# Storing a gathered row whole, in one run per partition, between two edge stages

## The reference

```
m1  = segment_sum(relu(x[src] + edge_attr), dst);             x = ln(x + (1 + eps) * x + m1)
l2  = 10 times f <- 0.9 * segment_sum(f[src] * ew, dst) + 0.1 * x;        x = ln(x + f)
h   = relu(x @ w1[r] + b1[r]) @ w2[r]
m3  = segment_sum(h[src, type] * norm, dst);                  x = ln(x + relu(m3 + b2))
e   = (x[dst] - x[src]) @ theta.T + tb + (x @ phi.T + pb)[src]
out = ln(x + segment_max(e, dst)), with 0 where a node has no edge
```

## Time and profile before

| what | value |
|---|---|
| device time, median of three runs | 4377.33 us (4374.49 to 4379.94) |
| span of the profiled execution | 4361.2 us |
| device time of that execution | not listed apart; the median is 16.1 us above the span |
| PE, DVE, ACT, POOL busy, share of the span | 56%, 66%, 31%, 60% |
| mean DMA rate | 128 GB/s |

### The profile page before, as it was taken

How to read it: one execution, slowest core, us unless ns; L and a number is a source line. 1 busy time by engine, 2 the same in 40 slices (tenths; PEclk the granted TensorE clock), 3 DMA queues, 4 the chain that set the end, 5 groups by cost and what they waited for, 6 DMA issues and landing times. The chain is left out here.

```text
span 4361.2 us, 60883 instructions
## 1 busy us (share of the span) xinstructions
PE 2429.7 (56%) x9482; PEld 1156.1 (27%) x9482; DVE 2868.7 (66%) x7411; ACT 1336.2 (31%) x4693; POOL 2603.5 (60%) x2544
## 2 busy tenths in 40 slices
PE   4720000677774888888886675642222106986564
PEld 2510000333331443344443221111111102333332
DVE  7989998788894888788887675323323144663333
ACT  0023333455552554455544221111000013431111
POOL 4747772666663777744444664756556604646776
PEclk9965555799997999899998897775555558995555
DMA  6647776899997866855553785224434242332111
GB/s 225 238 112 215 218 216 193 161 174 180 179 184 111 203 162 161 174 143 145 142 145 93 185 208 122 67 49 64 46 45 49 28 122 73 74 63 42 37 38 25
DMA packets 628412, 557.12 MB, mean 128 GB/s; under 512 B 379089, under 2 KB 548122, under 8 KB 623330
## 3 DMA queue, kind: packets, MB, share of 16 engines
q1 hardware_dynamic: 477606, 418.72, 35.7%
q0 software_dynamic: 90112, 95.44, 15.7%
q10 hardware_dynamic: 60612, 42.15, 4.6%
HBM read 291.63 MB, written 290.82 MB: 134 GB/s over the span
## 5 line engine op out<-in xcount | busy, mean ns | idle before, releaser
L1303 POOL DMA_INDIRECT out<-xob,ob x400 | 414.7, 1037 | 354.8 <-DVE xob L1415 246.8
L487 POOL DMA_INDIRECT xdst<-in_x,dstc x400 | 455.3, 1138 | 224.9 <-issue 135.0
L273 POOL DMA_INDIRECT gb<-nodes,ib x400 | 386.3, 966 | 258.0 <-ACT ib L851 141.6
L257 PE MATMUL bank<-ident,act 128*99 128x128 f32 x400 | 70.2, 302 | 657.9 <-ACT act L888 655.5
L273 POOL DMA_INDIRECT cgb<-layer,ib x160 | 175.4, 1096 | 232.4 <-ACT ib L2194 185.9
L293 PE MATMUL bank<-chosen,rec 128*6 128x512 bf16 x1200 | 309.2, 413 | 0.6 <-ACT packed L879 0.6
L1342 PE MATMUL bank<-hm,w 128*48 128x512 f32 x600 | 294.1, 629 | 0.0
L1359 PE MATMUL bank<-bxT,w 105*128 105x512 f32 x600 | 282.7, 607 | 8.5 <-ACT bxT L1246 8.5
L267 PE MATMUL bank<-ident,scan 99*128 99x99 f32 (+2 forms) x1120 | 200.2, 309 | 136.2 <-DVE scan L2013 101.5
L286 PE MATMUL bank<-l_chosen,l_rec 128*3 128x512 f32 x480 | 254.0, 679 | 0.5 <-DVE l_chosen L280 0.3
L273 POOL DMA_INDIRECT parent<-upper_rows,ib x176 | 175.3, 996 | 121.6 <-ACT ib L1271 57.1
(11 more groups left out here) (293 smaller groups left out, 6920.3 us busy)
## 6 DMA issues: line engine op xcount, KB each, us to landing
nodes<-wt SPq DMA_DIRECT2D x40, 1286.2 KB
edges<-gb ACTq DMA_DIRECT2D x100, 194.0 KB
upper_rows<-tb SPq DMA_DIRECT2D x100, 194.0 KB
xa<-upper_rows SPq DMA_DIRECT2D x100, 194.0 KB
lsb<-edges SPq DMA_DIRECT2D x100, 194.0 KB
run_rows<-upper_rows SPq DMA_DIRECT2D x100, 194.0 KB
deep_sum<-zeros SPq DMA_DIRECT2D x20, 960.0 KB
layer<-zeros SPq DMA_DIRECT2D x20, 960.0 KB
```

The source lines that it names most:

```text
L257: last = nc.tensor.transpose(slot(dst_ps[0:w, :], t), rows_sb[:, t, c0:c0 + w], ident[:, :])
L273: yield nc.gpsimd.indirect_dma_start(out=dst[s][:, t, 0:width], out_offset=None, in_=table, in_offset=bass.IndirectOffsetOnAxis(ap=ib[s][: ...
L487: nc.gpsimd.indirect_dma_start(out=xdst[:, k * F:(k + 1) * F], out_offset=None, in_=a["x"], in_offset=bass.IndirectOffsetOnAxis(ap=dstc[:, ...
L1303: nc.gpsimd.indirect_dma_start(out=out, out_offset=bass.IndirectOffsetOnAxis(ap=ob[s][:, t:t + 1], axis=0), in_=xo[s][:, t, :], in_offset= ...
```

## The change

The tensor `edges` grows from 51201 rows of 97 numbers to 51200 rows of 147. The store in `record` writes the gathered rows whole: 588 bytes a row, so 2352 bytes in one run per partition on both sides. The load in the second edge stage reads them whole into a buffer of the same width, and TensorE takes columns 48 to 143 of it. The views for the later stages stay at the front of the tensor.

```
-        edges = dram("edges", ((EP + 1) * PW,))
-        lone_rows = edges[0:EP * PW].rearrange("(e w) -> e w", w=PW)
+        edges = dram("edges", (EP * NW,))
+        lone_rows = edges.rearrange("(e w) -> e w", w=NW)
...
-        level_rows = [edges.rearrange("(e w) -> e w", w=PW), nodes[0:(EP + 1) * PW].rearrange("(e w) -> e w", w=PW),
+        level_rows = [edges[0:(EP + 1) * PW].rearrange("(e w) -> e w", w=PW), nodes[0:(EP + 1) * PW].rearrange("(e w) -> e w", w=PW),
...
-                        act.dma_start(cells(lone_rows, g, 0, 0, PW), gb[s][:, :, F:F + PW]).then_inc(s_lsw[s], 16)
+                        act.dma_start(rows(lone_rows, g), flat(gb[s])).then_inc(s_lsw[s], 16)
...
-            xa, ls, rt = st("xa", PW, U), st("lsb", PW, U), st("rt", 2 * F, U)
+            xa, ls, rt = st("xa", PW, U), st("lsb", NW, U), st("rt", 2 * F, U)
...
-                        sp.dma_start(ls[s][:, :, :], cells(lone_rows, g, 0, 0, PW)).then_inc(s_ls[s], 16)
+                        sp.dma_start(flat(ls[s]), rows(lone_rows, g)).then_inc(s_ls[s], 16)
...
-                        to_columns(psT, ls[s], XB).then_inc(s_cols, 1)
+                        to_columns(psT, ls[s], XB, F).then_inc(s_cols, 1)
```

## The result

The changed kernel takes 4338.7 us (median of four runs, 4334.0 to 4345.45) against 4375.91 us of four runs of the kernel before: ratio 0.9916, 95% interval 0.9903 to 0.9928, so 31 to 42 us less. The forecast was 4362; the range reached down to 4338. On three later chips the kernel before ran at 4362.13, 4355.98 and 4351.24 us, and the changed kernel, measured again beside the first of these, at ratio 0.9937 (0.9923 to 0.995): 27 us.

The account below looks back on a forecast made before the run. In the first edge stage VectorE's work and the loop of list stores, each awaiting the last landing, were taken as about equally long bounds. Span 4361.2 - 14.9 = 4346.3, plus 16.1 to the median, gave 4362; range 4338 to 4368.

Parts of the forecast that it names:

- part 3: First edge stage, after the store: fewer short writes let the list store land earlier; 14.9 us less, at best 39.6.
- The next thing late: First edge stage, once the list store lands early: TensorE's return of rows (12.4 us), then VectorE's own 5.0 us a piece.
- part 2: The row store's packets: 384 fewer, 102,400 bytes more; priced from quiet stretches, 0.89 against 0.81 us a piece, counted as nothing.
- Moving price: Row store in the first edge stage: 101 ns estimated for each 2352-byte packet, no gain or loss in pure moving.
- ScalarE's issue: Issue of the row store in the first edge stage: 549 to 355 ns, 19 us less ScalarE time, counted 0.
- the load: Second edge stage's load of stored rows: 0.24 us more a piece on SyncE's queue, hidden, counted 0.
- GpSimd: First edge stage: nothing added to its order; its buffer refill wait, some two pieces after the issue, shows no effect.
- B: Rival, first edge stage: bytes decide, each list store lands 0.29 us later; 20 to 29 us slower; 0.13 together with D.
- A: Rival, first edge stage: landing time fixed or gain reappears as TensorE waits; within 8.8 us of 4377; 0.30 with C.
- C: Rival, second edge stage: longer load holds TensorE, up to 13 us more, about 4375 in all; 0.30 together with A.
- D: Rival: store and load still cut by rows, packets stay, bytes grow, B's price applies; 0.13 together with B.

Follow-up runs that it names:

- 384-byte twin: Kernel before, with the unused 97th column left out of store and second-stage load: 512 runs of 384 bytes at multiples of 384; ratio 0.9931, on the last chip 0.9947.
- the load alone: Kernel before with its store kept, the second edge stage loading whole 588-byte rows of the node table instead of the stored rows; ratio 1.0008.

## Why the prediction held, and where it did not

*The bound and the place.* Right. The loop of list stores that each wait for the one before (part 3) was the place; its wait went from 80.9 to 0.9 us, VectorE's on it from 19.9 us in the whole stage to 1.4. The next thing late is the one named, TensorE's return of rows (12.4, now 16.8 us), and VectorE's own work.

*The size of part 3's term.* Too small. I took 14.9 us, the list wait of the steady part, and left the 5.0 us at the stage's end. That wait went too: in the whole stage 18.5 us of the list wait in all, and 4.0 us of the wait on the gathers (18.4 to 14.4), against 2.9 us more on TensorE (16.2 to 19.1). The sum, 19.6 us, comes near the 20.3 us by which the spans differ.

*From span to time.* A second error of the same sign. I put the 16.1 us between the span and the median into the sum as what lies around a span. In the runs of the changed kernel it is 2 us (4342.9 us with a span of 4340.9), so the profiled execution of the kernel before must have been one of about 4363 us, an estimate, faster than the runs that were timed. Timed, the gain was 37, 27 and, by the 384-byte twin on the last chip, 23 to 24 us; in the profiles the first edge stage is 17 to 25 us shorter (601 and 597.4 us before; 580.6 and 575.6 with the change, 572.8 with the twin). What made the kernel before slower in the first comparison's runs no profile shows; it stays open. That 4338.7 us lies in the range, 0.7 us above its lower end, is therefore partly luck: that end stood for TensorE's wait going with the others, and this wait grew; some 17 of the 37 us stand in no profile. The gain that was forecast, 15 us, was less than half of the 37.

*The cause inside part 3.* Wrong as I put it. I wrote of many short writes, and took the 384 packets that disappear as the reason. 512 runs of 384 or 512 bytes give the whole gain, 512 of 588 bytes lose it, and a move by 4 bytes undoes it with every run kept. What counts with 512 runs is whether they begin and end off multiples of 32 bytes. The change does not remove such ends: 2352 is 73.5 times 32, so in a table that begins at such a multiple each of its 128 runs has one end off it (an odd end). That makes 128 odd ends a store instead of 896, as of 512 runs of 388 bytes one in eight begins, and one in eight ends, at such a multiple. For the change itself this is the account that fits, not a test: its 128 runs were not moved, and how the cost grows between 128 and 896 was not tried. The second stage's store behind which I saw 37 GB/s fits it too: its rows of 384 bytes lie 772 bytes apart in DRAM, so they have the length of the fast store and not its place. It is the same in every run here, so what it costs is open.

*The length of a run.* The Trainium skill (DMA: Bandwidth & Descriptors, Specifications) wants at least 512 bytes for line rate and puts a read-modify-write below. Here 384-byte runs at multiples of 32 bytes took 21.7 ns a packet, and 512-byte runs 26.8 ns (16.3% of the engines over 50688 packets, 800 to 1320 us), nearly the same time per byte; with neither did SyncE wait more than 6 us for the list store, and with 588-byte runs at odd places it waited 112.5 us. The measurement decides against length as the test in this kernel. Whether a read-modify-write stands behind each odd end no run here shows.

The quiet prices of part 2 were read wrongly for this. 27.7 ns for 388 bytes are 14 bytes a ns, 63.9 ns for 1370 bytes are 21, so per byte there is a fall, though the line through the two longer packets gives 26 ns at 388 bytes and so shows no jump. And neither is the price of a store from the buffer: the 276 packets are those of a copy from DRAM to DRAM (L1173, issued at 2098.77 us), the 117 belong to loads of the second stage. In the first edge stage the 384-byte packets took 21.7 or 38.9 ns, by their place.

*Moving price.* 101 ns were expected for a packet of 2352 bytes; 16.2% of 16 x 520 us over 13536 packets, a ninth of them small, is 99.6 ns on average. Right within the mix. In the stage the move did get cheaper, where part 2 counted nothing: 16.2% of 520 us over 94 stores are 0.90 us a store, against 1.33 us before.

*ScalarE's issue, the load, GpSimd.* 355 ns expected, 338 measured, off the path as counted. The second stage changed by 1 us, as counted, and the load alone costs nothing that can be told from none.

*Rivals.* B (bytes decide) fell: 102 KB more came with a faster stage, and 301 KB more on top cost 8 to 15 us. A fell with the waits. C shows as at most 3 us. D fell with 144 packets a store.

## What to carry to other kernels

When a store of many rows runs beside transfers that others wait for, look at where its runs begin and end in DRAM before their number or length: pad or trim rows to a multiple of 32 bytes and begin the table at one (here 388 to 384 was enough), or join rows so that fewer ends are odd. Only part of the price stands at the store; the rest shows as longer packets of another queue and as late landings, so compare the queues' shares with and without it. And do not carry a profile's span to the median of other executions by a constant.

## What was not expected of the hardware

A table moved by 4 bytes changed the time of its own packets from 21.7 to 38.9 ns and that of another queue's unchanged transfers from 30.7% to 46.2% of the engines. Longer odd runs were no better: 588 bytes, 512 a store, with 102 KB more a piece, gave 1.004. And a DMA share slightly above 1 stood beside 175 GB/s in one kernel and 255 GB/s in another, so the share alone told nothing of how much more could be moved.
